# Attention values centred by VectorE and GpSimd instead of by a matrix product, and the gates' product laid on two halves of TensorE's columns

## The chip, the cores and the metric

The kernel runs on one core of a Trainium2 chip. The metric is the device time of one execution in microseconds (us). The kernel before takes 2300.62 us, the median of three runs (2298.52 to 2307.03).

## The reference

Two layers of attention and feed-forward over x of 16 x 256 x 512 with a context of the same shape. The change touches the first attention alone, an mLSTM form in which keys and values both are the context. What it computes, with 16 heads of 32:

```python
x = concatenate([q, k, v], -1)                       # q: layernorm(x); k = v = ctx_2048
ig, fg = x @ Wi + bi, x @ Wf + bf                    # the gates, 16 heads each
log_f = log_sigmoid(fg); log_f_cum = cumsum(log_f)   # "decays"
D = exp(log_D - max_log_D)                           # log_D from log_f_cum and ig, causal
C = (qh @ kh.T) / sqrt(32) * D
h = (C / (normalizer + EPS)) @ vh
mu = h.mean(-1); var = ((h - mu) ** 2).mean(-1)      # per head
hn = (h - mu) * rsqrt(var + EPS) * ln_scale
x = x + hn                                           # then the expert FFN, second attention, second FFN
```

Since h is linear in the values, subtracting from every value row its mean within each head (32 numbers) makes h come out with mean zero; the kernel centres the values and never the output.

## The kernel before

The program is written out by hand: each engine (TensorE as PE, VectorE as DVE, ScalarE as ACT, GpSimd as POOL, SyncE as SP for DMAs) walks the same list of stages, `order`, and issues its own part of each. Semaphores join them. An engine runs its instructions strictly in the order written.

The first of the kernel's stages holds attention and half of the expert FFN, software-pipelined over 16 batches of 256 tokens. `slots(b)` gives ten slots for each b. In them, batch `a = b` runs its attention core (`step`, `weighted`), batch `e = b-1` its normalisation and router, batch `f = b-2` the FFN (`gate_up`, `share`, `gate_low`, `down`), and batch `o = b+1` prepares its operands: `load`, `normalise_x`, `apply_x`, `turn_query`, `values`, `gates`, `decays`, `parts`, `norms`, `rows`. `operands(0)` does this for batch 0 ahead of the loop. The slots that matter here are, in the kernel before:

```python
yield [("step", a, 5), ("weighted", a, 3), ("normalise", e), ("values", o, 0), ("gate_low", f, 4), ...]
yield [("step", a, 6), ("weighted", a, 4), ("turn_x", e, 0), ("turn_x", e, 1), ("gates", o)]
yield [("step", a, 7), ("weighted", a, 5), ("gate_low", f, 5), ("values", o, 1), ("router", e),
       ("decays", o), ("down", f, 0), ("parts", o)]
yield [("step", a, 8), ("norms", o), ("weighted", a, 6), ("logits", e), ("down", f, 1), ...
```

Names and lines of the profile:

- `values` (PE L586, ACT L712): per batch two tiles of 128 tokens; four 128x128 f32 products each of the transposed context with the matrix `centring` (identity minus 1/32 within each head), which turn the context and centre it at once; ACT copies the result into `v_tok`.
- `gates` (PE L595): eight f32 products with 48 output partitions (16 input gates, 16 forget gates from partition 32) and 256 columns, summed in one bank; DVE L852, L853 and L855 read them and form |fg| in `la`; ACT L716 and L717 take exp and ln, each with a table load.
- `step` (PE L550 for scores, L561 and L563 for decays; ACT L733 exp; POOL L983 masks the exp; DVE L884 multiplies). `weighted` (PE L639, ACT L742).
- `gate_low` (ACT L278, DVE L302): makes the operand `a_t` of `down` (PE L162 to L164 with w_down).
- `decays` (DVE L863 to L868): a scan, a subtraction, a maximum scan, and `nm`, all on 16 partitions and with both inputs in SBUF. PE's `norms` (L603) waits for `nm`; `parts` (DVE L873, L876) feed PE's `rows` (L612).
- `sums` and `spread` (ACT L749, DVE L892 to L900, POOL L989 and L994) belong to the heads' normalisation; they use the tiles `us` and `hsq`.

An f32 product stands in the trace as two matmul instructions, so the 8 products of `gates` are 16 there. The trace groups many small SBUF tiles (`v_tok`, the transposed context, `e_t`) under the name `operands`, and `hsq`, `us`, `vm` stand under their own.

Of the kernel before, what the change touches and what calls it, by code (L numbers as in the profile page):

```python
# [15 lines left out]
P = 128  # L16
# [54 lines left out]
def build_program(nc, io, shapes):  # L71
# [26 lines left out]
    with main:  # L98
        named = {}

        def signal(name):
            if name not in named:
                named[name] = main.enter_context(nc.semaphore(name))
            return named[name]
# [63 lines left out]
        with both:  # L168
# [154 lines left out]
            with one:  # L323
                def sb1(name, shape, dt=F32):
                    return sbuf(one, name, shape, dt)

                GW = 32 + NH
                NI = NH // 4
# [6 lines left out]
                centring = sb1("centring", [P, P])  # L335
# [35 lines left out]
                va = sb1("va", [P, ST, NH])  # L371
                en_tok = [sb1(f"en_tok{i}", [P, ST, NH]) for i in range(2)]
# [24 lines left out]
                xr = io["x"].rearrange("(b t p) d -> b p t d", p=P, t=ST)  # L397
                ctr = io["ctx_t"].rearrange("(k p) n -> p k n", p=P)
# [36 lines left out]
                setup_made = signal("setup_made")  # L435
                pick_summed = signal("pick_summed")
# [13 lines left out]
                den_ready = signal("den_ready")  # L450
                h_squared = signal("h_squared")
# [10 lines left out]
                def operands(b):  # L462
                    return [("load", b), ("normalise_x", b), ("apply_x", b), ("turn_query", b, 0), ("turn_query", b, 1),
                            ("values", b, 0), ("gates", b), ("values", b, 1), ("decays", b), ("parts", b), ("norms", b),
                            ("rows", b)]

                def slots(b):
# [4 lines left out]
                    yield [("step", a, 2), ("weighted", a, 0), ("normalise_x", o), ("gate_low", f, 1), ("gate_up", f, 2),  # L472
# [5 lines left out]
                    yield [("step", a, 5), ("weighted", a, 3), ("normalise", e), ("values", o, 0), ("gate_low", f, 4),  # L478
                           ("gate_up", f, 5), ("share", f, 5)]
                    yield [("step", a, 6), ("weighted", a, 4), ("turn_x", e, 0), ("turn_x", e, 1), ("gates", o)]  # L480
                    yield [("step", a, 7), ("weighted", a, 5), ("gate_low", f, 5), ("values", o, 1), ("router", e),
# [21 lines left out]
                for name, b, *at in order:  # L503
                    if name in ("turn_query", "values", "turn_x"):
# [24 lines left out]
                def tensor_attention():  # L529
# [39 lines left out]
                    for name, b, *at in order:  # L569
# [10 lines left out]
                        elif name == "values":  # L580
                            t = at[0]
                            bank, filled, emptied, n = banks.at(name, b, t)
                            pe.wait_ge(emptied, n)
                            pe.wait_ge(c_loaded, 16 * (b + 1))
                            for k in range(KT):
                                ins = pe.run.matmul(bank_t[bank][:, k * P:(k + 1) * P], c_t[b % 2][:, k, t * P:(t + 1) * P],  # L586
                                                    centring[:, :], start=True, stop=True)
                            ins.then_inc(filled, 1)
                        elif name == "gates":
                            bank, filled, emptied, n = banks.at(name, b)  # L590
                            pe.wait_ge(emptied, n)
                            all_emptied("turn_query", b)
                            for k in range(2 * KT):
                                src = q_t[b % 2] if k < KT else c_t[b % 2]
                                ins = pe.run.matmul(bank_t[bank][0:GW, 0:S], w_if[:, k // KT, k % KT, :], src[:, k % KT, :],  # L595
                                                    start=(k == 0), stop=(k == 2 * KT - 1))
# [32 lines left out]
                        elif name == "weighted":  # L629
# [3 lines left out]
                            all_emptied("values", b)  # L633
# [50 lines left out]
                def scalar_attention():  # L684
# [4 lines left out]
                    for name, b, *at in order:  # L689
# [17 lines left out]
                        elif name == "values":  # L707
                            t = at[0]
                            bank, filled, emptied, n = banks.at(name, b, t)
                            act.wait_ge(filled, n + 1)  # L710
                            pair_filled(act, (b - 1) * PAIRS - 1)
                            act.run.copy(v_tok[b % 2][:, t, :, 0:DH], bank_t[bank].rearrange("p (h c) -> p h c", c=DH)  # L712
                                         ).then_inc(emptied, 1)
# [31 lines left out]
                        elif name == "sums":  # L745
                            bank, filled, emptied, n = banks.at("weighted", PAIRS - 1, b)
                            act.wait_ge(emptied, n + 1)
                            act.wait_ge(h_summed, b)
                            act.run.activation(hsq[:, :, :, :], h_t[:, :, :, 0:DH], ACT.Square).then_inc(h_squared, 1)  # L749
# [24 lines left out]
                def vector_attention():  # L774
# [6 lines left out]
                    dve.run.memset(centring[:, :], 0.0)  # L781
# [5 lines left out]
                    for i in range(P // DH):  # L787
                        ins = dve.run.memset(centring[i * DH:(i + 1) * DH, i * DH:(i + 1) * DH], -1.0 / DH)
                    dve.settle(ins)
                    dve.wait_ge(ident_made, 1)  # L790
                    dve.run.tensor_tensor(centring[:, :], centring[:, :], ident[:, :], ALU.add)
# [22 lines left out]
                    dve.run.tensor_tensor(w_router[1][:, :, :], wr_raw[:, :, :], w_router[0][:, :, :].bitcast(F32), ALU.subtract)  # L814
# [9 lines left out]
                    for name, b, *at in order:  # L824
# [23 lines left out]
                        elif name == "gates":  # L848
# [4 lines left out]
                            dve.run.tensor_scalar(ig[:, :], tb[0:NH, 0:S], b_if[0:NH, 0:1], None, ALU.add).then_inc(emptied, 1)  # L853
                            dve.wait_ge(emptied, n + 1)
                            dve.run.scalar_tensor_tensor(la[:, :], fg[:, :], -1.0, fg[:, :], ALU.mult, ALU.max  # L855
                                                         ).then_inc(decay_abs, 1)
# [1468 lines left out]
```

## Time and profile before

| | |
|---|---|
| median of 3 runs | 2300.62 us |
| profiled execution, its own time | 2303.52 us |
| its span in the trace | 2301.8 us |
| PE matmul busy | 2110.8 us, 92% |
| DVE, ACT, POOL busy | 1428.1, 779.0, 590.8 us |
| mean granted TensorE clock | 0.949 of full |

The stage that the change touches runs from the start to about 950 us. "Busy" is the time in which an engine has an instruction in flight; matmuls are pipelined, so what one costs on PE is the distance between starts and not its own length. "PEclk" is the granted clock of TensorE as a share of 2.4 GHz: 1.00 is that level, 0.50 is 1.2 GHz. In brackets behind a row stands the idle time of the engine ahead of it and who ended it.

### The profile page before, as it was taken

The numbers are of one execution on the slowest core, as the hardware profiler recorded it, in microseconds if no ns is written. First come the engines' busy times: TensorE is split into PE (matmuls) and PEld (weight loads), VectorE is DVE, ScalarE is ACT, GpSimd is POOL, SyncE is SP. The second block draws the span as 40 slices with busy tenths as digits, with TensorE's granted clock in tenths as the row PEclk, the third lists the DMA queues.
The fourth block names the chain that finished last, engine by engine and source line by source line (L and its number), as shares of the span: only waits on it lengthen the run. The fifth ranks groups of instructions, "written<-read, shape, count | busy, mean of one in ns | idle before, by whom it ended". The sixth has DMA issues, their size and how long they took to land. (4 is left out here: it accounts for less than half of the span.)

```text
span 2301.8 us, 36198 instructions
## 1 busy us (share of the span) xinstructions
PE 2110.8 (92%) x14438; PEld 1828.2 (79%) x14438; DVE 1428.1 (62%) x2819; ACT 779.0 (34%) x1484; POOL 590.8 (26%) x443
## 2 busy tenths in 40 slices
PE   5899999999999999879999999869999897988997
PEld 3788888888888889768888888757767777666887
DVE  4566677677667776545554444447886675684564
ACT  2343334334443333122222122135444454222332
POOL 1222222222222222100000000047675560002453
PEclk7589999999999999989999999989999996999999
DMA  2111111111111110411222221164453344224565
GB/s 75 60 46 43 38 38 38 38 38 38 38 38 38 38 38 31 136 46 56 74 74 67 68 68 65 37 236 124 133 156 119 122 153 163 78 98 159 146 160 85
DMA packets 106889, 189.54 MB, mean 82 GB/s; under 512 B 13474, under 2 KB 34018, under 8 KB 105698
## 3 DMA queue, kind: packets, MB, share of 16 engines
q1 hardware_dynamic: 99330, 170.13, 22.4%
q0 software_dynamic: 7392, 17.11, 3.7%
q8 instruction: 114, 1.87, 0.3%
q14 instruction: 53, 0.43, 0.1%
HBM read 119.33 MB, written 67.95 MB: 81 GB/s over the span
## 5 line engine op out<-in xcount | busy, mean ns | idle before, releaser
L1331 PE MATMUL psum<-kv,toep 128*128 128x288 f32 x1280 | 328.6, 419 | 42.1 <-ACT yx L1379 24.3
L1331 PEld LDWEIGHTS psum<-kv,toep 128*128 128x128 f32 x1280 | 249.4, 196 | 118.8 <-ACT yx L1379 30.4
L162 PE MATMUL psum<-xn_t_h,w_gate_h 128*128 128x256 f32 x768 | 234.1, 305 | 19.4 <-DVE xn_t_l L1153 5.5
L983 POOL TENSOR_SCALAR_AFFINE_SELECT operands<-operands 128x512 f32<-128x512 f32 x128 | 83.7, 654 | 603.3 <-ACT operands L733 603.2
L163 PE MATMUL psum<-xn_t_l,w_up_h 128*128 128x256 f32 x768 | 218.3, 284 | 0.0
L162 PE MATMUL psum<-xn_t_h,w_up_h 128*128 128x256 f32 x768 | 218.3, 284 | 0.0
L164 PE MATMUL psum<-xn_t_h,w_gate_l 128*128 128x256 f32 x768 | 218.1, 284 | 0.0
L163 PE MATMUL psum<-xn_t_l,w_gate_h 128*128 128x256 f32 x768 | 217.8, 284 | 0.0
L164 PE MATMUL psum<-xn_t_h,w_up_l 128*128 128x256 f32 x768 | 217.5, 283 | 0.0
L639 PE MATMUL psum<-operands 128*128 128x33 f32 x1536 | 211.6, 291 | 0.0
L639 PEld LDWEIGHTS psum<-operands 128*128 128x128 f32 x1536 | 197.2, 205 | 16.8 <-issue 5.8
L270 ACT ACTIVATE th<-psum 128x256 f32<-128x256 f32 x192 | 73.7, 384 | 372.5 <-PE psum L164 372.5
L159 POOL TENSOR_TENSOR rstd<-rstd,minus_half 128x2 f32<-128x2 f32 x48 | 35.0, 730 | 597.4 <-DVE rstd L155 597.4
L286 DVE SCALAR_TENSOR_TENSOR th<-th,psum 128x256 f32<-128x256 f32 x192 | 80.5, 419 | 167.0 <-ACT th L270 166.2
L162 PEld LDWEIGHTS psum<-xn_t_h,w_gate_h 128*128 128x128 f32 x768 | 148.4, 193 | 27.5 <-issue 19.2
L1488 POOL TENSOR_TENSOR terms<-yx,qx 128x768 f32<-128x768 f32 x64 | 133.9, 2093 | 127.3 <-ACT yx L1379 127.3
L162 PE MATMUL psum<-w_down_h,a_t_h 128*128 128x512 f32 x384 | 154.8, 403 | 7.1 <-DVE x_all L317 7.1
L302 DVE TENSOR_TENSOR a_t_l<-th,a_t_h 128x256 fp32r<-128x256 f32 x192 | 81.6, 425 | 123.1 <-ACT a_t_h L278 122.6
L164 PE MATMUL psum<-w_down_h,a_t_l 128*128 128x512 f32 x384 | 151.5, 394 | 0.0
L163 PE MATMUL psum<-w_down_l,a_t_h 128*128 128x512 f32 x384 | 151.4, 394 | 0.0
L278 ACT CAST a_t_h<-th 128x256 fp32r<-128x256 f32 x192 | 78.4, 408 | 212.5 <-DVE th L294 212.5
L162 PEld LDWEIGHTS psum<-xn_t_h,w_up_h 128*128 128x128 f32 x768 | 148.5, 193 | 0.0
(299 smaller groups left out, 5065.7 us busy)
## 6 DMA issues: line engine op xcount, KB each, us to landing
toep<-ssm_padded_scratch SPq DMA_DIRECT2D x64, 256.0 KB, 3.5
kx<-in_ctx_pairs SPq DMA_DIRECT2D x32, 384.0 KB, 4.2
x_scratch<-x_all SPq DMA_DIRECT2D x21, 512.0 KB, 2.8
x_all<-in_x SPq DMA_DIRECT2D x16, 512.0 KB, 3.8
operands<-in_ctx_t SPq DMA_DIRECT2D x16, 512.0 KB, 4.9
xn_scratch<-xn SPq DMA_DIRECT2D x16, 512.0 KB, 2.8
x_all<-xn_scratch SPq DMA_DIRECT2D x16, 512.0 KB, 4.4
xn_t_scratch<-operands SPq DMA_DIRECT2D x16, 512.0 KB, 2.9
```

The costliest lines, as they stand in the source:

```text
L159: pool.run.tensor_tensor(rstd[:, at:at + n], rstd[:, at:at + n], minus_half[:, 0:n], ALU.pow).then_inc(ln_inverse, 1)
L162: pe.run.matmul(out, lhs[0], rhs[0], start=first, stop=False)
L163: pe.run.matmul(out, lhs[0], rhs[1], start=False, stop=False)
L164: return pe.run.matmul(out, lhs[1], rhs[0], start=False, stop=last)
L270: act.run.activation(th[jl % 2][:, :], bank_t[bank][:, 0:S], ACT.Tanh, scale=0.5).then_inc(gate_tanh, 1)
L278: act.run.copy(a_t[0][:, jl, :], th[jl % 2][:, :]).then_inc(act_high, 1)
L286: dve.settle(dve.run.scalar_tensor_tensor(tj, tj, 1.0, t4, ALU.add, ALU.mult))
L302: dve.run.tensor_tensor(a_t[1][:, jl, :], tj, a_t[0][:, jl, :].bitcast(F32), ALU.subtract).then_inc(act_low, 1)
L639: ins = pe.run.matmul(hv[:, st, j, :], c[:, j, blk * P:(blk + 1) * P], v_tok[b % 2][:, tt, 2 * p + j, :], start=(blk != 1), stop=(blk != 2))
L983: pool.run.affine_select(out=diag, in_=diag, compare_op=ALU.is_ge, fill=0.0, base=0, pattern=[[0, 2], [0, 2], [1, P]], channel_multiplier= ...
L1331: ins = pe.run.matmul(out, w[:, (o - k) * P:(o - k + 1) * P], pairs, start=(k == 0), stop=(k == o))
L1488: pool.run.tensor_tensor(window(terms[n % 2][:, :, :, :], 5, [[HR * HR, KB], [HR, HR], [1, 3]]), window(yx[n % 2][:, :, :], 3, [[44, KB], ...
```

## The change

The context's rows (tokens by channels) are given to the kernel as a further input. For each batch SP loads them (512 KB) into `us` (batch 0) or `hsq` (all others), in a new stage `load_values` in slot 2. DVE sums each head and scales by 1/32 (`sum_values`, slot 5). POOL subtracts the mean and writes `v_tok` (`values`, now one stage in slot 7). The products with `centring`, their bank, ACT's copies and the setup of `centring` go.

The eight products of the gates alternate between columns 0 to 47 and 64 to 111 of the array, each half summing four of them; DVE adds the two halves with two more instructions.

```diff
                 def operands(b):
-                    return [("load", b), ("normalise_x", b), ("apply_x", b), ("turn_query", b, 0), ("turn_query", b, 1),
-                            ("values", b, 0), ("gates", b), ("values", b, 1), ("decays", b), ("parts", b), ("norms", b),
+                    return [("load", b), ("load_values", b), ("normalise_x", b), ("apply_x", b), ("turn_query", b, 0),
+                            ("turn_query", b, 1), ("gates", b), ("sum_values", b), ("values", b), ("decays", b), ("parts", b), ("norms", b),
                             ("rows", b)]
...
-                    yield [("step", a, 5), ("weighted", a, 3), ("normalise", e), ("values", o, 0), ("gate_low", f, 4),
+                    yield [("step", a, 5), ("weighted", a, 3), ("normalise", e), ("sum_values", o), ("gate_low", f, 4),
...
-                    yield [("step", a, 7), ("weighted", a, 5), ("gate_low", f, 5), ("values", o, 1), ("router", e),
+                    yield [("step", a, 7), ("weighted", a, 5), ("gate_low", f, 5), ("values", o), ("router", e),
```

On PE, in the order of the program: `values` and `gates`, and the wait in `weighted`.

```diff
-                        elif name == "values":
-                            t = at[0]
-                            bank, filled, emptied, n = banks.at(name, b, t)
-                            pe.wait_ge(emptied, n)
-                            pe.wait_ge(c_loaded, 16 * (b + 1))
-                            for k in range(KT):
-                                ins = pe.run.matmul(bank_t[bank][:, k * P:(k + 1) * P], c_t[b % 2][:, k, t * P:(t + 1) * P],
-                                                    centring[:, :], start=True, stop=True)
-                            ins.then_inc(filled, 1)
                         elif name == "gates":
...
+                            pe.wait_ge(c_loaded, 16 * (b + 1))
                             for k in range(2 * KT):
                                 src = q_t[b % 2] if k < KT else c_t[b % 2]
-                                ins = pe.run.matmul(bank_t[bank][0:GW, 0:S], w_if[:, k // KT, k % KT, :], src[:, k % KT, :],
-                                                    start=(k == 0), stop=(k == 2 * KT - 1))
+                                at_ = k % 2 * GROUP
+                                ins = pe.run.matmul(bank_t[bank][at_:at_ + GW, 0:S], w_if[:, k // KT, k % KT, :],
+                                                    src[:, k % KT, :], start=(k < 2), stop=(k >= 2 * KT - 2),
+                                                    tile_position=(0, at_))
...
-                            all_emptied("values", b)
+                            pe.wait_ge(values_ready, b + 1)
```

On ACT the copy of `values`, and a wait ahead of the square into `hsq`; then DVE in `gates` and in the new stage.

```diff
-                            act.run.copy(v_tok[b % 2][:, t, :, 0:DH], bank_t[bank].rearrange("p (h c) -> p h c", c=DH)
-                                         ).then_inc(emptied, 1)
...
+                            act.wait_ge(values_ready, min(b + 2, B))
...
-                            dve.run.tensor_scalar(ig[:, :], tb[0:NH, 0:S], b_if[0:NH, 0:1], None, ALU.add).then_inc(emptied, 1)
+                            dve.settle(dve.run.tensor_scalar(ig[:, :], tb[0:NH, 0:S], b_if[0:NH, 0:1], None, ALU.add))
+                            dve.run.tensor_tensor(fg[:, :], fg[:, :], tb[GROUP + 32:GROUP + GW, 0:S], ALU.add)
+                            dve.run.tensor_tensor(ig[:, :], ig[:, :], tb[GROUP:GROUP + NH, 0:S], ALU.add).then_inc(emptied, 1)
...
+                        elif name == "sum_values":
+                            dve.wait_ge(values_loaded, 16 * (b + 1))
+                            dve.wait_ge(values_ready, b)
+                            dve.settle(dve.run.tensor_reduce(vm[:, :, :], raw_values(b)[:, :, :, :], AX, ALU.add))
+                            dve.run.tensor_scalar(vm[:, :, :], vm[:, :, :], 1.0 / DH, None, ALU.mult).then_inc(values_summed, 1)
```

On GpSimd, and on SP, the new stages:

```diff
+                        elif name == "values":
+                            pool.wait_ge(values_summed, b + 1)
+                            pair_filled(pool, (b - 1) * PAIRS - 1)
+                            pool.run.tensor_tensor(v_tok[b % 2][:, :, :, 0:DH], raw_values(b)[:, :, :, :],
+                                                   vm[:, :, :].unsqueeze(3).broadcast_to([P, ST, NH, DH]), ALU.subtract
+                                                   ).then_inc(values_ready, 1)
...
+                        elif name == "load_values":
+                            if b == 1:
+                                sp.wait_ge(setup_made, 1)
+                                sp.wait_ge(router_split, 1)
+                            elif b:
+                                sp.wait_ge(h_summed, b - 1)
+                            if b:
+                                sp.wait_ge(values_ready, b)
+                            sp.run.dma_start(raw_values(b)[:, :, :, :], vr[b]).then_inc(values_loaded, 16)
```

How the instructions stand, first on GpSimd, from the fourth `step` of a batch to the first of the next. Before (L983 masks, L989 is `sums`):

```order
L983 AFFINE_SELECT operands<-operands 128x2x256 x2
L159 TENSOR_TENSOR rstd<-rstd,minus_half 128x2
L983 AFFINE_SELECT operands<-operands 128x2x256 x4
L989 TENSOR_TENSOR us<-h_t,ln_s 128x1024
L983 AFFINE_SELECT operands<-operands 128x2x256
```

Now, with the mask at L989, the values at L982 and `sums` at L996:

```order
L989 AFFINE_SELECT operands<-operands 128x2x256 x2
L159 TENSOR_TENSOR rstd<-rstd,minus_half 128x2
L989 AFFINE_SELECT operands<-operands 128x2x256 x3
L982 TENSOR_TENSOR operands<-hsq,vm 128x32x32
L989 AFFINE_SELECT operands<-operands 128x2x256
L996 TENSOR_TENSOR us<-h_t,ln_s 128x1024
L989 AFFINE_SELECT operands<-operands 128x2x256
```

The four masks in a row were those of steps 5, 6, 7 and the next batch's step 0; the subtraction now stands right behind the mask of step 7.

On VectorE, from the gates to `nm` (slots 6 and 7 with `gate_low` of the FFN between). Before:

```order
L852 TENSOR_SCALAR fg<-psum,b_if 16x256
L853 TENSOR_SCALAR ig<-psum,b_if 16x256
L855 SCALAR_TENSOR_TENSOR la<-fg 16x256
L884 SCALAR_TENSOR_TENSOR operands<-psum,operands 128x768
L302 TENSOR_TENSOR a_t_l<-th,a_t_h 128x256
L863 SCALAR_TENSOR_TENSOR la<-fg,la 16x256
```

Now:

```order
L845 TENSOR_SCALAR fg<-psum,b_if 16x256
L846 TENSOR_SCALAR ig<-psum,b_if 16x256
L847 TENSOR_TENSOR fg<-fg,psum 16x256
L848 TENSOR_TENSOR ig<-ig,psum 16x256
L850 SCALAR_TENSOR_TENSOR la<-fg 16x256
L884 SCALAR_TENSOR_TENSOR operands<-psum,operands 128x768
L302 TENSOR_TENSOR a_t_l<-th,a_t_h 128x256
L863 SCALAR_TENSOR_TENSOR la<-fg,la 16x256
```

Two additions come in ahead of `la`; everything behind stands as it did.

On TensorE, slot 7 from `weighted` of pair 5 to the router. Before:

```order
L639 MATMUL psum<-operands 128x33 x6
L586 MATMUL psum<-centring,operands 128x128 x4
L162 MATMUL psum<-xn_t_h,w_router_h 32x256
L163 MATMUL psum<-xn_t_l,w_router_h 32x256
L164 MATMUL psum<-xn_t_h,w_router_l 32x256
```

Now:

```order
L643 MATMUL psum<-operands 128x33 x6
L162 MATMUL psum<-xn_t_h,w_router_h 32x256
L163 MATMUL psum<-xn_t_l,w_router_h 32x256
L164 MATMUL psum<-xn_t_h,w_router_l 32x256
```

The products with `centring` are gone from between, as they are in slot 5.

## Rows read from the trace of the kernel before

**Rows 1.** Stretches: us, PE busy (instructions), PEclk, DMA share, GB/s.

```profile
300.00:900.00 600.00, 600.00 (x5201) 1.00 0.11 38
```

**Rows 2.** Timeline of PE, one batch: start us, us, engine, line, operation.

```profile
513.37 3.65 PE L595 MATMUL psum<-operands,w_if 128*48 128x256 f32 x16
516.96 0.48 PE L550 MATMUL psum<-operands 32*128 32x256 f32 x2
...
519.17 1.14 PE L586 MATMUL psum<-centring,operands 128*128 128x128 f32 x8
520.06 0.36 PE L162 MATMUL psum<-xn_t_h,w_router_h 128*32 128x256 f32 x1
...
524.96 0.39 PE L162 MATMUL psum<-w_down_h,a_t_h 128*128 128x512 f32 x1
...
525.73 0.92 PE L550 MATMUL psum<-operands 32*128 32x256 f32 x8
526.57 0.26 PE L603 MATMUL psum<-ident,nm 16*128 16x16 f32 x2
```

**Rows 3.** Timeline of DVE in the same batch.

```profile
517.07 0.47 DVE L852 TENSOR_SCALAR fg<-psum,b_if 16x256 f32<-16x256 f32 x1 [2.04 <-PE psum L595]
...
518.06 0.41 DVE L855 SCALAR_TENSOR_TENSOR la<-fg 16x256 f32<-16x256 f32 x1
...
523.34 0.42 DVE L302 TENSOR_TENSOR a_t_l<-th,a_t_h 128x256 fp32r<-128x256 f32 x1 [4.00 <-ACT a_t_h L278]
523.69 0.41 DVE L863 SCALAR_TENSOR_TENSOR la<-fg,la 16x256 f32<-16x256 f32 x1
...
526.01 0.41 DVE L868 SCALAR_TENSOR_TENSOR nm<-fg,gm 16x256 f32<-16x256 f32 x1
```

**Rows 4.** Timeline of ACT in the same batch.

```profile
521.97 0.81 ACT L733 ACTIVATE operands<-psum 128x768 f32<-128x768 f32 x1
```

**Rows 5.** Timeline of POOL in the same batch.

```profile
522.85 0.64 POOL L983 TENSOR_SCALAR_AFFINE_SELECT operands<-operands 128x512 f32<-128x512 f32 x1 [10.09 <-ACT operands L733]
```

**Rows 6.** Timeline of DVE in an early batch.

```profile
133.59 0.74 DVE L868 SCALAR_TENSOR_TENSOR nm<-fg,gm 16x256 f32<-16x256 f32 x1
```

**Rows 7.** Timeline of POOL at the same time.

```profile
133.42 0.64 POOL L983 TENSOR_SCALAR_AFFINE_SELECT operands<-operands 128x512 f32<-128x512 f32 x1 [9.30 <-ACT operands L733]
```

**Rows 8.** Single lines: count, duration ns min/median/max, first and last start us.

```profile
L989 POOL TENSOR_TENSOR us<-h_t,ln_s x16: 2161/2194/2198, 91.8 to 918.3; 128x1024 f32<-128x1024 f32 x16
...
L895 DVE TENSOR_SCALAR den<-den x16: 181/2126/2130, 90.3 to 922.3; 128x32 f32<-128x32 f32 x16
...
L899 DVE TENSOR_REDUCE va<-hsq x16: 1208/1212/1214, 93.8 to 924.0; 128x32 f32<-128x1024 f32 x16
```

**Rows 9.** Timeline of PE where it waited, an early batch and two later stages.

```profile
134.48 0.27 PE L603 MATMUL psum<-ident,nm 16*128 16x16 f32 x2 [1.34 <-DVE nm L868]
...
1554.06 2.18 PE L1331 MATMUL psum<-kv,toep 128*128 128x288 f32 x8 [2.62 <-DMA toep<-ssm_padded_scratch]
...
1721.98 2.70 PE L1331 MATMUL psum<-kv,toep 128*128 128x288 f32 x7 [2.25 <-ACT yx L1379]
```

**Rows 10.** Stretches of PE behind such places, columns as in rows 1.

```profile
245.40:248.50 3.10, 3.10 (x27) 1.00 0.00 0
248.50:251.90 3.40, 3.40 (x10) 0.50 0.00 0
135.90:146.00 10.10, 10.10 (x52) 0.50 0.03 10
1554.00:1558.00 4.00, 3.94 (x16) 1.00 0.18 65
1723.10:1726.40 3.30, 3.30 (x9) 0.50 0.09 37
```

**Rows 11.** Timeline of PE ahead of the loop, batch 0.

```profile
19.59 2.08 PE L586 MATMUL psum<-centring,operands 128*128 128x128 f32 x8 [0.68 <-ACT operands L705]
22.35 5.75 PE L595 MATMUL psum<-operands,w_if 128*48 128x256 f32 x16 [0.68 <-ACT operands L712]
```

More of the change, by code:

```diff
@@ L327, in build_program @@
                 GW = 32 + NH
+                GROUP = 64
                 NI = NH // 4
@@ L334, in build_program @@
                 merge_f = sb1("merge_f", [3 * NE, 1])
-                centring = sb1("centring", [P, P])
                 row_of = sb1("row_of", [GW, 2, 3, P], BF16)
@@ L371, in build_program @@
                 va = sb1("va", [P, ST, NH])
+                vm = sb1("vm", [P, ST, NH])
                 en_tok = [sb1(f"en_tok{i}", [P, ST, NH]) for i in range(2)]
@@ L397, in build_program, with raw_values @@
                 xr = io["x"].rearrange("(b t p) d -> b p t d", p=P, t=ST)
+                vr = io["ctx"].rearrange("(b t p) (h c) -> b p t h c", p=P, t=ST, h=NH)
+                def raw_values(b):
+                    return hsq if b else us
                 ctr = io["ctx_t"].rearrange("(k p) n -> p k n", p=P)
@@ L435, in build_program @@
                 setup_made = signal("setup_made")
+                router_split = signal("router_split")
                 pick_summed = signal("pick_summed")
@@ L450, in build_program @@
                 den_ready = signal("den_ready")
+                values_loaded = signal("values_loaded")
+                values_summed = signal("values_summed")
+                values_ready = signal("values_ready")
                 h_squared = signal("h_squared")
@@ L471, in slots @@
                            ("share", f, 1)]
-                    yield [("step", a, 2), ("weighted", a, 0), ("normalise_x", o), ("gate_low", f, 1), ("gate_up", f, 2),
+                    yield [("step", a, 2), ("weighted", a, 0), ("load_values", o), ("normalise_x", o), ("gate_low", f, 1), ("gate_up", f, 2),
                            ("share", f, 2)]
@@ L503, in build_program @@
                 for name, b, *at in order:
-                    if name in ("turn_query", "values", "turn_x"):
+                    if name in ("turn_query", "turn_x"):
                         banks.plan((name, b, at[0]), (7, 5)[at[0]] if name == "turn_x" else 6)
@@ L706, in scalar_attention @@
                                          bank_t[bank].rearrange("p (k n) -> p k n", k=KT)).then_inc(emptied, 1)
[L707 to L711, printed above, removed]
-                            act.run.copy(v_tok[b % 2][:, t, :, 0:DH], bank_t[bank].rearrange("p (h c) -> p h c", c=DH)
-                                         ).then_inc(emptied, 1)
                         elif name == "gates":
@@ L780, in vector_attention @@
                     dve.run.memset(row_of[:, :, :, :], 0.0)
-                    dve.run.memset(centring[:, :], 0.0)
                     for v in v_tok:
@@ L786, in vector_attention @@
                     dve.wait_ge(setup_zeroed, 1)
[L787 to L791, printed above, removed]
                     dve.wait_ge(patterns_made, 2)
@@ L813, in vector_attention @@
                     dve.wait_ge(router_high, 1)
-                    dve.run.tensor_tensor(w_router[1][:, :, :], wr_raw[:, :, :], w_router[0][:, :, :].bitcast(F32), ALU.subtract)
+                    dve.run.tensor_tensor(w_router[1][:, :, :], wr_raw[:, :, :], w_router[0][:, :, :].bitcast(F32), ALU.subtract
+                                          ).then_inc(router_split, 1)
                     dve.wait_ge(pick_summed, 1)
@@ L988, in gpsimd_attention @@
                             pool.wait_ge(gate_w_loaded, 64)
+                            pool.wait_ge(values_ready, 1)
                             pool.run.tensor_tensor(us[:, :, :, :], h_t[:, :, :, 0:DH],
@@ L2298 @@
         "x": a["x"].reshape(T, D),
-        "ctx_t": ctx_t,
+        "ctx": ctx, "ctx_t": ctx_t,
         "ctx_pairs": np.concatenate([pairs, pairs[..., 0:4]], axis=-1).reshape(CH, 128, -1),
```

## The prediction, as put on record before the changed kernel ran

> **What bounds the kernel now.** I read the stretches first. From 300 to 900 us PE has an instruction in flight all the time, at the full 2.4 GHz [rows 1]: in the touched stage PE sets the time, and what leaves PE is gained as long as nothing makes PE wait. So the second view is the timeline of one batch on every engine, to see how much room each hand-over to PE has. All rooms but one are wide. The narrow one is `norms` (L603). PE reaches it at 526.57, right behind the scores that start at 525.73 [rows 2]; `nm`, which it needs, ends at 526.01 + 0.41 = 526.42 [rows 3]. The two arrive together, with at most 0.1 us to spare. In an early batch PE already waited 1.34 us there [rows 9].
>
> Both ways to `norms` start at the end of the gates, which I call G (516.96, where the next PE work starts [rows 2]). PE's way takes 526.57 - 516.96 = 9.61 us: step 7, `weighted`, centring products, router, `down`, scores. The other way is a chain: DVE's gates and `la`, ACT's exp, table load, ln, table load, then step 7's exp at 521.97 [rows 4], GpSimd's mask and `a_t_h`, DVE's `a_t_l` at 523.34, `decays` from 523.69 to 526.42 [rows 3]. It takes 9.46 us to `nm`, about 9.6 until PE can start. The change shortens the first way and lengthens the second.
>
> **The change part by part, for one batch of the loop.**
>
> Centring products: the second group takes PE from 519.17 to 520.06 [rows 2], 0.89 us; the first has the same eight instructions, so 1.78 us leave PE per batch. ACT's two copies go too; ACT has idle time, nothing is gained there.
>
> Gates: 16 instructions from 513.37 to 516.96 are 3.59 us, 0.224 each [rows 2]. The trace has no product on two column halves. The nearest row has two row groups: step 8's eight score instructions, four of 256 and four of 128 columns, would take 4 x 0.224 + 4 x 0.112 = 1.34 us one after the other, and take 525.73 to 526.57, 0.84 us [rows 2]. That fits an array in which the second instruction of one product runs beside the first of the next, while the two instructions of one product follow each other. Put on the gates, that makes 9 steps for 16: 9 x 0.224 = 2.02 us. Bounds: 3.59 (no overlap) and 8 x 0.224 = 1.79. I take 2.02, so 1.57 leave PE.
> The Trainium skill ("TensorE: Matmul & The Clock Gate", Part 3: Packing small matmuls) says that column tiles overlap about as well as row tiles, the span being one matmul and a few ns per further tile; by that the gates would take 1.8 us and each batch 0.2 us less than I take.
>
> DVE after the gates: L852 to L855 start 0.99 us apart, two instructions [rows 3]; two more of the same size put `la` 0.95 later. This lies on the chain.
>
> DVE's sum: like L899, 1.21 us [rows 8], and 0.2 for the scale, in slot 5. DVE idles 4.00 us before `a_t_l` and 2.04 before the gates [rows 3], so I cost it at nothing; with that cover gone it would be 1.4. The load is 512 KB in slot 2, used in slot 5; DMA is busy 0.11 of the time [rows 1]: nothing. SP has behind it the store of the normalised rows, which comes three slots later; if SP were held up until then it would delay no PE work of that batch. ACT's new wait in `sums` is for a subtraction that ends two slots earlier: nothing.
>
> GpSimd's subtraction: two SBUF inputs and 1024 elements as L989, 2.19 us [rows 8]. GpSimd is idle there, but not alone. It stands right behind the mask of step 7, which ends at 522.85 + 0.64 = 523.49 [rows 5], and DVE's `decays`, each with both inputs in SBUF, begin at 523.69 [rows 3]. Rows show what such a pair does: L868 started at 133.59 while the mask from 133.42 ran, and took 0.74 instead of 0.41 us, ending with it [rows 6, 7, 3]; L895, a 32-element operation that takes 0.18 at its least, takes 2.13 beside L989 [rows 8]. Bounds for the block on the chain: nothing, if GpSimd gets its turn only when the chain is done, and 2.19. GpSimd asks at 523.46, while `a_t_l` runs, before L863 asks; even if L863 came first, each of the next four instructions waits for the one ahead and leaves a gap. So I take nearly all of it, 2.05.
> The Trainium skill ("SBUF — State Buffer", Summary: rules for kernel authors) states the same against this change: with two SBUF inputs on VectorE the second of the two engines to issue is blocked until the first ends. By that the block is the whole subtraction, 2.19, and each batch 0.14 us longer than I take.
>
> The balance at `norms`: PE's way is 9.61 - 0.89 = 8.72. The chain is 9.6 + 0.95 + 2.05 = 12.6. PE waits 3.9 us, of which some 0.7 fall earlier, before the last third of `down` (524.96), since `a_t_l` is 0.95 later and PE 0.89 earlier [rows 2, 3]. Without the block it would wait 1.8. Behind `norms`, DVE's `parts` have several us until `rows`, and move with it.
>
> So PE's time per batch: -1.78 - 1.57 + 3.9 = +0.5 us. That alone would be 7 us over 13 batches: the gain is eaten by the wait.
>
> The clock: the wait falls into a stretch in which PE has only scores, `norms` and `weighted`. Before, that stretch without a wait (245.4 to 248.5) kept 1.00, and once 0.50 followed for 3.4 us [rows 10]. After 1.34 us of waiting there in the early batch, 0.50 followed from 135.9 to 146 [rows 9, 10]. After a wait of 2.25 elsewhere it fell for 3.3 us, after one of 2.62 it did not [rows 9, 10]. With 3.9 us I expect a fall to 1.2 GHz in every batch. Price: at half clock half the stretch is lost, 1.7 us for 3.4, 5 for 10. The stretch begins partly inside the wait and lasts some us into the next `down`; I take 2.9, from 1.6 to 5.
>
> Batches: the operands of 3 to 15 are made beside FFN work, 13 times: 13 x (0.5 + 2.9) = 44 us. One fall of the clock (1.7) was there already. Batch 0: the first centring product and its copy go, 22.35 - 19.59 = 2.8 us, gates 5.75 to about 3.3 [rows 11], against 0.95 and part of a block: 3 us gained; batches 1 and 2, at low clock, half a us each. Sum: 44 - 2 - 4 = +38 us on the span of 2301.8, so 2340; 1.7 lie outside the span, and the profiled execution stands 2.9 above the median, so 2339.
>
> **The rivals.**
>
> B, the halves do not overlap: all as above, but the 1.57 stays on PE (and 2.5 in batch 0). 2339 + 20 + 4 = 2363. For it: no row shows column halves. Against: the row groups overlap.
>
> C, the wait comes but the clock holds: 13 x 0.5 - 4 = +2, 2303. For it: the wait of 2.62 us without a fall [rows 9, 10]. Against: that one lay between long dense products, this one lies in thin work.
>
> D, GpSimd does not block the chain, but the shorter wait of 1.8 lets the clock fall: 13 x (-3.35 + 1.8 + 1.6 to 2.9) - 6 = -5 to +12, 2295 to 2312.
>
> E, the other side: the two ways to `norms` do not diverge by more than the 1.8, because the subtraction slips between or behind `decays`, and the clock holds. Then 13 x (-3.35 + 1.8) - 4 = -24, 2276. The place is the same: PE's wait for `nm` per batch; as long as it and the clock's loss stay below 3.35 us together, the kernel is faster. For it: DVE has idle time elsewhere. Against: rows 6 to 8.
>
> **How the numbers follow.** My forecast A 0.46, B 0.16, C 0.12, D 0.14, E 0.12. A's own range is 2322 to 2366, from the clock's bounds. The range 2290 to 2368 leaves out E and the top of B and A. A difference of 0.5% (2289 to 2312) is what a measurement can tell. Faster: E and a bit of D and C, 0.15. Same: C and most of D, 0.2. Slower: A, B and D's top, 0.65.
>
> **What would show it.** PE waits for `nm` at `norms` by 3 to 4 us in batches 3 to 15; the first instruction of `decays` that meets the subtraction lasts over 2 us; the 16 gate instructions take about 2.0 us; the granted clock falls to 0.5 once per batch behind `norms`, where it was 1.00. Wrong: waits under 2 us with `decays` at their old durations (E, D), gates still at 3.6 (B), or a clock that stays at 1.00 through the waits (C).

## The result, and the profile after

The changed kernel takes 2339.40 us, the median of four runs (2335.89 to 2341.97); runs of the kernel before beside it, 2303.82. The ratio is 1.015, 95% interval 1.012 to 1.019: slower by about 36 us, where 2339 was forecast. The profiled execution took 2335.89 us with a span of 2334.0.

The page's first part and its clock line, to be held against the table of before:

```profile
PE 2097.9 (90%) x14182; PEld 1815.1 (78%) x14182; DVE 1489.0 (64%) x2877; ACT 761.3 (33%) x1452; POOL 623.2 (27%) x459
...
PEclk9989999999999999989999999989999997899999
```

PE has 256 instructions less and the kernel is slower. The mean clock, 0.949, is what it was (before, the low stretches lay in the first 150 us), so the page alone does not show the cause. The stretches do; columns as in rows 1:

```profile
300.00:900.00 600.00, 565.76 (x4687) 495.93 (x4687) 441.47 (x934) 209.66 (x423) 163.51 (x131) 0.93 0.13 45
```

This row also has PEld, DVE, ACT and POOL between PE and the clock. In 600 us PE now has 34 us with nothing in flight and a clock of 0.93, against none and 1.00 [rows 1]. The waits of PE from 150 to 940 us: who waited for whom, us in total, times, longest.

```profile
PE psum L607 <- DVE nm L868: 34.3, 13, 2.6
...
PE psum L162 <- DVE a_t_l L302: 6.8, 13, 0.5
```

Thirteen batches, two waits in each, at the two places named. PE's timeline in one batch, to be read against [rows 2]:

```profile
526.54 1.93 PE L598 MATMUL psum<-operands,w_if 128*48 128x256 f32 x16
528.40 0.48 PE L560 MATMUL psum<-operands 32*128 32x256 f32 x2
...
530.62 0.28 PE L162 MATMUL psum<-xn_t_h,w_router_h 128*32 128x256 f32 x1
...
536.16 0.50 PE L162 MATMUL psum<-w_down_h,a_t_h 128*128 128x512 f32 x1 [0.53 <-DVE a_t_l L302]
...
537.06 0.92 PE L560 MATMUL psum<-operands 32*128 32x256 f32 x8
540.62 0.26 PE L607 MATMUL psum<-ident,nm 16*128 16x16 f32 x2 [2.65 <-DVE nm L868]
540.82 2.54 PE L643 MATMUL psum<-operands 128*128 128x33 f32 x12
...
543.63 0.80 PE L162 MATMUL psum<-w_down_h,a_t_h 128*128 128x512 f32 x1
```

The gates take 1.86 us, `weighted` follows step 7 without the centring products, and then PE waits 0.53 and 2.65. From the end of the gates to `norms` it is 12.22 us, where it was 9.61. Without the centring products PE's way would be 8.72, so between starts the waits cost 12.22 - 8.72 = 3.50 us. The idle time in the rows, 3.18, is less: an instruction ahead of a wait is in flight for 0.39 us, where the next would start after 0.23. DVE and POOL in the same batch, to be read against [rows 3, 5]:

```profile
528.52 0.47 DVE L845 TENSOR_SCALAR fg<-psum,b_if 16x256 f32<-16x256 f32 x1 [0.34 <-PE psum L598]
...
530.40 0.41 DVE L850 SCALAR_TENSOR_TENSOR la<-fg 16x256 f32<-16x256 f32 x1
...
535.68 0.43 DVE L302 TENSOR_TENSOR a_t_l<-th,a_t_h 128x256 fp32r<-128x256 f32 x1 [3.88 <-ACT a_t_h L278]
536.02 2.13 DVE L863 SCALAR_TENSOR_TENSOR la<-fg,la 16x256 f32<-16x256 f32 x1
...
540.06 0.41 DVE L868 SCALAR_TENSOR_TENSOR nm<-fg,gm 16x256 f32<-16x256 f32 x1
```

```profile
535.18 0.64 POOL L989 TENSOR_SCALAR_AFFINE_SELECT operands<-operands 128x512 f32<-128x512 f32 x1 [9.26 <-ACT operands L730]
535.80 2.09 POOL L982 TENSOR_TENSOR operands<-hsq,vm 128x1024 f32<-128x1024 f32 x1
```

The subtraction starts while `a_t_l` runs; the first operation of `decays` then lasts 2.13 us instead of 0.41, and ends 0.26 after the subtraction. The line over all batches: count, duration ns min/median/max.

```profile
L863 DVE SCALAR_TENSOR_TENSOR la<-fg,la x16: 414/2130/2132, 28.0 to 891.0; 16x256 f32<-16x256 f32 x16
```

The clock behind the wait, columns as in rows 1:

```profile
541.10:547.90 6.80, 6.80 (x24) 0.50 0.00 0
```

Such a stretch follows the wait in each of the 13 batches, 6.8 us long or 10.2.

A batch, taken from one start of the first scan of `decays` to the next and averaged over batches 3 to 14, lasts 59.06 us; before, most lasted 55.75. I use this period below. What left PE (1.78 + 1.73) and what the waits cost (3.50) cancel: 55.75 - 3.51 + 3.50 = 55.74. The 3.3 us above that are the clock's.

### The profile page after: what moved, and what is told of

Read it like the earlier page. It is cut to its first block and busy times, and to the rows that moved or that the text cites. A ratio compares the mean times of both kernels' runs of the same rounds, so it can differ in the third digit from the quotient of the medians.

```text
span 2334.0 us, 35804 instructions
## 1 busy us (share of the span) xinstructions
PE 2097.9 (90%) x14182; PEld 1815.1 (78%) x14182; DVE 1489.0 (64%) x2877; ACT 761.3 (33%) x1452; POOL 623.2 (27%) x459
## 5 line engine op out<-in xcount | busy, mean ns | idle before, releaser
L989 POOL TENSOR_SCALAR_AFFINE_SELECT operands<-operands 128x512 f32<-128x512 f32 x128 | 83.3, 650 | 596.3 <-ACT operands L730 596.0
L643 PE MATMUL psum<-operands 128*128 128x33 f32 x1536 | 230.1, 306 | 0.0
L643 PEld LDWEIGHTS psum<-operands 128*128 128x128 f32 x1536 | 215.3, 221 | 17.0 <-issue 6.0
L162 PE MATMUL psum<-w_down_h,a_t_h 128*128 128x512 f32 x384 | 167.6, 437 | 13.9 <-DVE x_all L317 7.1
L163 PE MATMUL psum<-w_down_l,a_t_h 128*128 128x512 f32 x384 | 160.6, 418 | 0.0
L164 PE MATMUL psum<-w_down_h,a_t_l 128*128 128x512 f32 x384 | 159.9, 416 | 0.0
L163 PEld LDWEIGHTS psum<-xn_t_l,w_up_h 128*128 128x128 f32 x768 | 148.4, 193 | 0.0
```

What stands on the lines that cost most here:

```text
L162: pe.run.matmul(out, lhs[0], rhs[0], start=first, stop=False)
L163: pe.run.matmul(out, lhs[0], rhs[1], start=False, stop=False)
L164: return pe.run.matmul(out, lhs[1], rhs[0], start=False, stop=last)
L643: ins = pe.run.matmul(hv[:, st, j, :], c[:, j, blk * P:(blk + 1) * P], v_tok[b % 2][:, tt, 2 * p + j, :], start=(blk != 1), stop=(blk != 2))
L989: pool.run.affine_select(out=diag, in_=diag, compare_op=ALU.is_ge, fill=0.0, base=0, pattern=[[0, 2], [0, 2], [1, P]], channel_multiplier= ...
```

## The experiments

The ratios below are against runs of the kernel before made beside each group of experiments. Their medians are 2298.82 us for the first four experiments, 2301.28 for order_only_after, all_moved, order_only_before and halves_in_turn, and 2304.86 for gate_low_moved and norms_moved.

My theory: PE's wait for `nm` ate what PE saved, and the fall of the granted clock behind that wait made the kernel slower. The rivals: the time follows the work on PE and something in the new parts is dear; or the load of the rows, or a thinner stage, slows everything.

**One part alone.** First the gates' halves on the kernel before, with VectorE's two additions as in the change:

```diff
+                                at_ = k % 2 * GROUP
-                                ins = pe.run.matmul(bank_t[bank][0:GW, 0:S], ..., start=(k == 0), stop=(k == 2 * KT - 1))
+                                ins = pe.run.matmul(bank_t[bank][at_:at_ + GW, 0:S], ..., start=(k < 2), stop=(k >= 2 * KT - 2),
+                                                    tile_position=(0, at_))
```

> The kernel before with the gates' product on two column halves and VectorE's two additions, the centring products left on PE. Theory W (a wait for nm at norms, and the clock falling behind it): PE saves 1.73 us per batch at the gates (3.59 to 1.86), nm comes 0.93 us later against PE's unchanged way, so PE waits 0.9 us per batch at norms: net -0.8 per batch. If 0.9 us of waiting is enough for the granted clock to fall in every batch (3 us each), the kernel takes about 2330; if it holds, about 2290. Rival P (the time follows the amount of work on PE, waits hide nothing): -1.7 per batch, 2278.

Measured: 2315.47 us, ratio 1.008 (1.006 to 1.011), slower with less work on PE. Its waits from 150 to 900 us and PE behind one of them:

```profile
PE psum L606 <- DVE nm L873: 10.4, 13, 0.8
```

```profile
527.92 0.26 PE L606 MATMUL psum<-ident,nm 16*128 16x16 f32 x2 [0.80 <-DVE nm L873]
528.11 2.22 PE L642 MATMUL psum<-operands 128*128 128x33 f32 x12
...
530.60 0.80 PE L162 MATMUL psum<-w_down_h,a_t_h 128*128 128x512 f32 x1
```

The first products of `down` are 0.42 apart there, where they are 0.23 at the full clock. Between starts this wait costs 0.89 us: from the gates to `norms` it is 10.50 us, where it was 9.61. Batch 3, the only one with the wait and without a fall, has a period of 54.93 us, and 55.75 - 1.73 + 0.89 is 54.91. Where the clock falls for 6.8 us the period is 58.03, so such a stretch costs 3.1. A wait of 0.8 us was thus followed by a fall in 12 of 13 batches. Rival P is out. The time lies between the two sums of the expectation: the clock held behind `norms` of batch 3 and fell for only 3.4 us in batch 4, and up to the period of batch 5 the kernel had gained some 8 us.

Then the values alone, the changed kernel with the gates in one piece and without the two additions:

```diff
-                                ins = pe.run.matmul(bank_t[bank][at_:at_ + GW, 0:S], ..., tile_position=(0, at_))
+                                ins = pe.run.matmul(bank_t[bank][0:GW, 0:S], ..., start=(k == 0), stop=(k == 2 * KT - 1))
-                            dve.run.tensor_tensor(fg[:, :], fg[:, :], tb[GROUP + 32:GROUP + GW, 0:S], ALU.add)
-                            dve.run.tensor_tensor(ig[:, :], ig[:, :], tb[GROUP:GROUP + NH, 0:S], ALU.add).then_inc(emptied, 1)
```

> The changed kernel with the gates' product back in one piece of 48 columns and without VectorE's two additions. Theory W: PE saves 1.78 us per batch, its way to norms is 8.7 us, the chain is 9.6 plus the block of 1.72 that the changed kernel shows, so PE waits 2.6 us per batch; with the clock falling (3 us) the balance is +3.8 per batch, 13 times, less some 3 us ahead of the loop: about 2350, slower than the full change. Rival P (the halves or the additions do the harm): below 2339, down to 2280.

Measured: 2328.99 us, ratio 1.014 (1.012 to 1.016). Its waits:

```profile
PE psum L605 <- DVE nm L864: 33.0, 13, 2.5
```

The wait is the expected one. The time is 21 us below 2350. The clock fell in each batch, but in 9 of 13 for 3.4 us only (a period of 58.10 us), not 6.8 (59.6), which is some 13 of the 21. I had priced the fall as a constant, and it is not one. Nor is this kernel slower than the full change, as I had expected from that price.

**The subtraction's place.** The changed kernel with `values` behind `sum_values` in slot 5:

```diff
-                    yield [("step", a, 5), ("weighted", a, 3), ("normalise", e), ("sum_values", o), ("gate_low", f, 4),
+                    yield [("step", a, 5), ("weighted", a, 3), ("normalise", e), ("sum_values", o), ("values", o), ("gate_low", f, 4),
...
-                    yield [("step", a, 7), ("weighted", a, 5), ("gate_low", f, 5), ("values", o), ("router", e),
+                    yield [("step", a, 7), ("weighted", a, 5), ("gate_low", f, 5), ("router", e),
```

> The changed kernel with GpSimd's subtraction moved from slot 7 to slot 5, behind the sums. Theory W with the block: the first operation of decays is back at 0.41 us, PE's wait at norms falls from about 3.2 to 1.5 (with the part ahead of the last third of down 1.8). If the clock still falls in each batch but for a shorter stretch, about 2305 to 2315; if it holds, 2280. Rival (VectorE is not held by GpSimd but by something else, such as the load of the rows): the first operation of decays still lasts 2.13 and the time stays near 2339.

Measured: 2298.99 us, ratio 1.000 (0.999 to 1.001); 40 us below the full change, 35 by the ratios. DVE in one batch, and PE's waits:

```profile
517.55 0.41 DVE L863 SCALAR_TENSOR_TENSOR la<-fg,la 16x256 f32<-16x256 f32 x1
```

```profile
PE psum L607 <- DVE nm L868: 11.9, 13, 0.9
...
PE psum L162 <- DVE a_t_l L302: 6.8, 13, 0.5
```

The operation is back at 0.41 us with the rows still loaded, so GpSimd held it and the load did not. The wait at `norms` fell by 1.72 us per batch, just what the block had added. The clock still fell in each batch, but for 6.8 and 3.4 us in turn. The mean period is 56.42 us, 2.64 below that of the full change: the block is 1.72 of it, and the other 0.9 is the clock, which fell for less time behind the shorter wait.

**The clock by itself.** The changed kernel with dense products in PE's wait; their results are not used:

```diff
                             pe.wait_ge(emptied, n)
+                            if b >= 3:
+                                for i in range(22):
+                                    pe.run.matmul(bank_t[bank][:, 0:S], w_gate[0][:, i % KT, 0:P], xn_t1[0][:, i % KT, :],
+                                                  start=True, stop=True)
                             pe.wait_ge(norm_log, b + 1)
```

> The changed kernel with 22 additional products of 128x128 by 256 columns on PE, ahead of its wait for nm, in each batch from the third on; their results are thrown away. They last about 2.6 us, as long as the wait. Theory W with the clock: the wait is full of dense work, the granted clock stays at 1.00 in the loop, and the 3 us per batch that weighted and down lose at 1.2 GHz come back: about 2300. Rival (the clock costs nothing here, the chain alone sets the time): 2339 or more.

Measured: 2297.63 us, ratio 0.999 (0.998 to 1.001). More work on PE, the same chain, the same block (2.13 us), and 42 us less, 37 by the ratios. Its stretch:

```profile
300.00:900.00 600.00, 594.75 (x5235) 0.99 0.14 47
```

Behind `norms` the clock held in all 13 batches; in two of them it fell some 10 us later, for 3.4 us. The usual period is 55.91, so the clock had cost at least 59.06 - 55.91 = 3.15 us per batch. This is the run that tells my forecast from its case C: with the clock held, the change is worth next to nothing in either direction.

**Room at the wait.** If the chain is the trouble, an order that gives it room should bring the saved work out. The changed kernel with `gate_low` of the last piece ahead of the gates, so that `decays` no longer stand behind `a_t_l`, and `norms` two stages later:

```diff
-                    yield [("step", a, 6), ("weighted", a, 4), ("turn_x", e, 0), ("turn_x", e, 1), ("gates", o)]
-                    yield [("step", a, 7), ("weighted", a, 5), ("gate_low", f, 5), ("values", o), ("router", e),
+                    yield [("step", a, 6), ("weighted", a, 4), ("turn_x", e, 0), ("turn_x", e, 1), ("gate_low", f, 5), ("gates", o)]
+                    yield [("step", a, 7), ("weighted", a, 5), ("values", o), ("router", e),
...
-                    yield [("step", a, 8), ("norms", o), ("weighted", a, 6), ("logits", e), ("down", f, 1),
+                    yield [("step", a, 8), ("weighted", a, 6), ("logits", e), ("norms", o), ("down", f, 1),
```

> The changed kernel with two stages moved: gate_low of the last FFN piece from slot 7 to slot 6, ahead of the gates, and norms behind weighted and logits of slot 8. GpSimd's subtraction stays in slot 7. Theory W: decays no longer stand behind a_t_l, which waited for ACT's exp of step 7, so they start some 3 us earlier, end before the subtraction begins, and nm is ready before PE wants it; the waits of 0.5 and 2.65 us go and with them the fall of the clock. Per batch 55.8 - 1.8 - 1.7 = 52.2 us, 13 to 15 times: about 2250. Rival X (VectorE, ACT or the thinner stretch of PE bind somewhere else once this wait is gone): 2275 to 2300, with waits at another line or the clock at half behind norms as before.

Measured: 2258.44 us, ratio 0.981 (0.979 to 0.984). From 150 to 860 us PE waits for nothing. The clock still fell behind `norms` in 4 of 13 batches, for 3.4 us, at 1.6 us each (periods of 53.7 for 52.14); that is most of the 8 us above the expected 2250. The subtraction still overlaps DVE, now in `parts`:

```profile
499.09 2.07 POOL L982 TENSOR_TENSOR operands<-hsq,vm 128x1024 f32<-128x1024 f32 x1
```

```profile
499.62 0.69 DVE L317 TENSOR_TENSOR x_all<-x_all,psum 128x512 f32<-128x512 f32 x1 [0.23 <-PE psum L164]
500.22 1.08 DVE L873 CAST parts<-gm 48x256 bf16<-48x256 f32 x1
```

The cast lasts 1.08 instead of 0.28 us and PE does not come to wait for it: here a block costs only where the chain is tight. The addition at L317, with one input in PSUM, keeps its length (0.69 us; 0.67 without the subtraction beside it). The same with the subtraction in slot 5 too:

```diff
+                    yield [..., ("sum_values", o), ("values", o), ("gate_low", f, 4), ...]
...
+                    yield [("step", a, 7), ("weighted", a, 5), ("router", e),
```

> As the one before, and GpSimd's subtraction in slot 5. Theory W: the chain has room already, so the subtraction's place no longer matters: the same time within 0.3%, about 2250. Rival Y (the block still reaches PE, through parts and rows): 10 to 25 us faster than with the subtraction in slot 7.

Measured: 2254.39 us, ratio 0.979 (0.977 to 0.982), 0.2% from the one before, with the same usual period of 52.14 us: its place no longer matters. And the two moves on the kernel before, without the change:

```diff
-                    yield [("step", a, 6), ..., ("turn_x", e, 1), ("gates", o)]
-                    yield [("step", a, 7), ("weighted", a, 5), ("gate_low", f, 5), ("values", o, 1), ("router", e),
+                    yield [("step", a, 6), ..., ("turn_x", e, 1), ("gate_low", f, 5), ("gates", o)]
+                    yield [("step", a, 7), ("weighted", a, 5), ("values", o, 1), ("router", e),
...
-                    yield [("step", a, 8), ("norms", o), ("weighted", a, 6), ("logits", e), ("down", f, 1),
+                    yield [("step", a, 8), ("weighted", a, 6), ("logits", e), ("norms", o), ("down", f, 1),
```

> The kernel before with the same two stages moved and nothing else. Theory W: PE did not wait there, so room is made and not used: the same as before, about 2299, within 0.3%. Rival Z (the order itself is the gain, by a better clock or a tighter PE): 2280 or less.

Measured: 2305.80 us, ratio 1.001 (1.000 to 1.003). Room alone gives nothing. So the change and the room are worth 43 us together (2301.28 to 2258.44), and neither is worth anything alone.

Each move by itself on the changed kernel, first that of `gate_low`:

```diff
-                    yield [("step", a, 6), ("weighted", a, 4), ("turn_x", e, 0), ("turn_x", e, 1), ("gates", o)]
-                    yield [("step", a, 7), ("weighted", a, 5), ("gate_low", f, 5), ("values", o), ("router", e),
+                    yield [("step", a, 6), ("weighted", a, 4), ("turn_x", e, 0), ("turn_x", e, 1), ("gate_low", f, 5), ("gates", o)]
+                    yield [("step", a, 7), ("weighted", a, 5), ("values", o), ("router", e),
```

> The changed kernel with only gate_low of the last FFN piece moved from slot 7 to slot 6, ahead of the gates; norms stay where they were. In the run with both moves nm was done 7.7 us after the end of the gates, and PE's way to norms is 8.7 us, so if that move is the one that matters there is no wait left: the same as with both, about 2256. Rival (PE needs norms moved too): a wait of 1 us or more at norms in each batch and about 2280 or more.

Measured: 2252.49 us, ratio 0.977 (0.974 to 0.979): this one move is enough, and it is the fastest version run, 2.3% below the kernel before. One batch on DVE and PE:

```profile
546.10 0.41 DVE L863 SCALAR_TENSOR_TENSOR la<-fg,la 16x256 f32<-16x256 f32 x1 [1.22 <-ACT la L714]
548.42 0.75 DVE L868 SCALAR_TENSOR_TENSOR nm<-fg,gm 16x256 f32<-16x256 f32 x1
```

```profile
549.32 0.29 PE L607 MATMUL psum<-ident,nm 16*128 16x16 f32 x2
```

`decays` now wait for ln alone. `nm` is there at 549.17, PE comes at 549.32 and does not idle. A mask on GpSimd from 548.26 to 548.90 makes the last operation 0.75 us long, and this almost takes up the room.

Then that of `norms`:

```diff
-                    yield [("step", a, 8), ("norms", o), ("weighted", a, 6), ("logits", e), ("down", f, 1),
+                    yield [("step", a, 8), ("weighted", a, 6), ("logits", e), ("norms", o), ("down", f, 1),
```

> The changed kernel with only norms moved, behind weighted and logits of slot 8. The chain to nm keeps its 12.2 us, PE's way grows from 8.7 to 10.6, so a wait of 0.5 us ahead of the last third of down and one of about 1.1 at norms stay, 1.6 for 3.2; the clock falls in each batch (3 us) as with the 0.8 us of the run with the gates alone: 52.1 + 1.6 + 3 = 56.7 per batch, about 2305. Rival (a wait so much later in thin work no longer moves the clock): about 2270.

Measured: 2297.11 us, ratio 0.997 (0.995 to 0.998). Its waits:

```profile
PE psum L607 <- DVE nm L868: 12.3, 13, 1.0
...
PE psum L162 <- DVE a_t_l L302: 6.8, 13, 0.5
PE psum L162 <- DVE x_all L317: 2.2, 9, 0.2
```

1.5 us of waiting per batch stay at the two places, as expected, and 0.2 us at a third one in 9 batches. The clock fell in 9 of 13 batches, for 3.4 or 6.8 us, less than I had put in, so the time is 8 us below my 2305.

**What lets two column halves overlap.** As with all moved, but the query's four products go to one half and then the context's four to the other:

```diff
-                                at_ = k % 2 * GROUP
+                                at_ = k // KT * GROUP
...
-                                                    src[:, k % KT, :], start=(k < 2), stop=(k >= 2 * KT - 2),
+                                                    src[:, k % KT, :], start=(k % KT == 0), stop=(k % KT == KT - 1),
```

> As all_moved, but the four products with the query go to the first column half and then the four with the context to the second, instead of alternating. If two products run side by side only when they stand next to each other in the queue, only the one at the seam does, the gates take about 3.4 us instead of 1.86, and the kernel some 15 x 1.5 = 23 us more than all_moved, about 2273. If the order did not matter, the same as all_moved.

Measured: 2277.21 us, ratio 0.990 (0.987 to 0.993), 23 us above all_moved as expected, but not for the whole reason. The gates on PE, to the start of step 7:

```profile
500.82 2.83 PE L598 MATMUL psum<-operands,w_if 128*48 128x256 f32 x16
503.58 0.48 PE L560 MATMUL psum<-operands 32*128 32x256 f32 x2
```

They take 2.76 us, not 3.4. The starts read as follows: the first half's first four instructions run alone; then one with the longer first step of a new sum starts 0.006 us behind the fifth, and from there four run beside four; the second half's last four are alone again. So the second half did not wait until the first half's last instruction had started. That is 0.9 us per batch, 14 in all; most of the rest is the clock, which fell here for 3.4 us in each of 11 batches in a row (from 186 to 736 us) without any wait. Why here and not in all_moved, with five such stretches over the loop, stays open.

## Why the prediction was right

**The place.** Every step that it named showed: PE's wait at `norms` in batches 3 to 15, the smaller one ahead of the last third of `down`, the long first operation of `decays`, and the clock at 0.5 behind it. Undoing the block (values_early) and holding the clock (filled_wait) each gave back 35 to 40 us; the two overlap, since the shorter wait also shortened the falls of the clock. Room at the one wait (gate_low_moved) turned the change to 2.3% faster.

**The terms.** The centring products went as priced. The gates came out at 1.86 us, not 2.02: the step that was mis-sized is the reading of the scores, from which I took that one product's second instruction runs beside the next one's first. In the trace two products start 0.007 us apart and run beside each other throughout, in eight pairs, mostly 0.216 apart. The scores of the kernel before do the same: two row groups start 0.006 us apart, four pairs of instructions in 0.84 us. The Trainium skill's span model ("TensorE: Matmul & The Clock Gate", Part 3: Packing small matmuls), which I had set aside for 0.2 us more, was the better one. DVE's two additions: 530.40 - 528.52 is 1.88 where it was 0.99, so 0.89 for my 0.95. The block: 2.13 - 0.41 = 1.72, not 2.05; the subtraction takes 2.09, not 2.19, it had begun 0.22 us before the blocked operation, and this one ends 0.26 behind it. I had misread the rows on that last point: L868 does not end with the mask but 0.27 later (134.33 for 134.06 [rows 6, 7]), so part of its own 0.41 us lies outside the block. The wait, counted between starts as in my sum, was 3.50 and not 3.9, from the last two errors: 12.6 - 0.06 - 0.33 = 12.2 for the chain. My 1.8 without the block was right: 10.50 - 8.72 in values_early.

**The clock.** I took 2.9 us per batch. The balance says 59.06 - 55.74 = 3.3. The batch shown, with a stretch of 6.8, loses 1.1 us in `weighted` and 2.0 in `down` (6.31 for 4.31 us), 3.1 together, and every third batch had a stretch of 10.2. So the wait was 0.4 too long in my sum and the clock 0.4 too short, and the two cancel. That the sum came within 1 us of the median is luck in part: this, and that the runs of before beside it stood 3 us higher than the ones I worked from. In ratios I forecast 1.017 and 1.015 was measured; on the span I forecast +38 and it grew by 32.2.

**Ahead of and behind the loop.** From the start to batch 2 the changed kernel gained 5.7 us, for my 4; from the last batch's scan to the end it is 2.3 us shorter, which I had not foreseen. Loop: +40.2. Together 32.2, the difference of the spans.

**The rivals.** B fell with the gates at 1.86 us. D and E fell with the 2.13 us; values_early is D made on purpose, and it came out in D's range (2295 to 2312). C fell with the clock, and filled_wait is close to C made on purpose: 2298 for 2303.

## What to carry to other kernels

Before work is taken off the bounding engine, look at every place where it meets another engine and read how much room there is; where there is none, the work taken away ahead of that place becomes a wait, and what lengthens the other side comes on top. Then give the room first: here one moved stage turned 1.5% slower into 2.3% faster, though moving it together with `norms` gave the kernel before nothing (moving it alone there was not tried). Here a wait in thin TensorE work was paid twice, once as a wait and again in the granted clock, and since the wait (3.50 us) only took back what PE had saved (3.51), the second price, 3.3 us per batch, was the whole loss.

## What the runs showed of the hardware

- 0.80 us of waiting, in a stretch where TensorE has only small products, was followed in 11 of 13 batches by 6.8 us at 1.2 GHz, which cost 3.1 us, nearly four times the wait. With the wait filled by dense products the clock held behind it in all 13.
- Without a wait the same stretch mostly kept the clock: in 12 of 13 batches of the kernel before, in all of gate_low_moved, 9 of order_only_after, 8 of all_moved, but only 2 of halves_in_turn. So the wait is not the only thing that lets it fall, and what else does was not found.
- How long the clock stays low is not set by the wait: after 2.5 us it was mostly 3.4, after 0.8 nearly always 6.8, after 3.2 it was 6.8 or 10.2.
- Two f32 products on columns 0 to 47 and 64 to 111 run side by side at full overlap (16 instructions in 1.86 us for 3.59). With all of one half ahead of the other half, four of the eight instructions of each still overlap (2.76 us).
- GpSimd's subtraction, which started 0.12 us behind VectorE's `a_t_l`, held VectorE's next operation in all 13 batches (2.13 us for 0.41). It holds a VectorE cast of one SBUF input (1.08 us for 0.28) as it does an operation with two, but not an addition with one input in PSUM (0.69 us for 0.67).
